# A recurrent block in 64 slots a chunk: turns, statistics and outputs at other slots, and the next chunk's normalising on ScalarE

## The reference

```python
xn = layernorm(x)                                   # over 512, eps 1e-5
q, k, v = xn @ Wq.T, xn @ Wk.T, xn @ Wv.T           # 128 wide
# per step t:  r_t = q_t @ M.T;  M = 0.99 * M + v_t.T @ k_t / 4
s = (r @ Wo.T) * sigmoid(gate)
h = layernorm(xn) * gamma + beta
y = silu(h @ dequant(fc1_q, fc1_scales) + b1)       # 512 -> 2048, scales per group of 128
z = y @ dequant(fc2_q, fc2_scales) + b2             # 2048 -> 512
g = silu(xn + 0.5 * z)
out = x + s * g
```

## Time and profile before

| | before |
|---|---|
| median of 3 runs | 1263.76 us (1263.1 to 1264.02) |
| the profiled execution | 1263.97 us, its span 1262.1 us |
| PE busy | 1196.1 us, 95% |
| DVE busy | 1135.1 us, 90% |
| ACT busy | 916.6 us, 73% |
| POOL busy | 777.7 us, 62% |
| chain that ended last | PE 77%, DVE 10%, ACT 7%, issue 4% |
| granted PE clock | 0.985 of full speed over the span |

### The profile page before, as it was taken

The page is one execution under the profiler, slowest core; times in us unless marked ns, Lnnn a source line. Parts: engine busy times, 40 slices in busy tenths (PEclk is TensorE's granted clock), DMA queues, the critical chain, the costliest instruction groups (busy, mean ns, idle before and its releaser), DMA issues.

```text
span 1262.1 us, 18951 instructions
## 1 busy us (share of the span) xinstructions
PE 1196.1 (95%) x6028; PEld 618.3 (49%) x6028; DVE 1135.1 (90%) x1965; ACT 916.6 (73%) x1590; POOL 777.7 (62%) x766
## 2 busy tenths in 40 slices
PE   2799999999999999999999999999999999999994
PEld 1344555545555554555555455555545545555551
DVE  7799899999998999999898999999898999999887
ACT  6688677777767777776777777777786777778673
POOL 6067747749474783947569384765947477494732
PEclk9799999999999999999999999999999999999997
DMA  9511130402103030120302112040210304020011
GB/s 331 182 35 34 26 76 1 101 1 65 37 15 86 1 94 8 49 53 3 99 1 68 34 38 64 1 100 2 67 34 20 82 1 101 1 59 9 26 43 35
DMA packets 41620, 65.68 MB, mean 52 GB/s; under 512 B 11696, under 2 KB 11952, under 8 KB 41008
## 3 DMA queue, kind: packets, MB, share of 16 engines
q1 hardware_dynamic: 41232, 64.36, 19.1%
q10 hardware_dynamic: 288, 0.08, 0.0%
HBM read 47.59 MB, written 16.81 MB: 51 GB/s over the span
## 4 chain that ended last, share of the span: by engine, by line
PE 77%; DVE 10%; ACT 7%; issue 4%; POOL 1%; DMA 1%; SPq 0%; ACTq 0%; DVEq 0%
PE blk L492 29%; PE blk L510 27%; PE side L452 6%; PE side L477 4%; PE side L441 3%; DVE blk L772 3%; ACT blk L638 2%; PE side L428 2%; DVE g_lo L742 2%; DVE tops L810 1%; ACT z_rows L664 1%; DVE y_split L763 1%; DVE y_split L758 1%; PE side L470 1%; PE side L471 1%
## 5 line engine op out<-in xcount | busy, mean ns | idle before, releaser
L772 DVE TENSOR_TENSOR blk<-blk,ratio_rows 128x512 f32<-128x512 f32 x960 | 647.8, 690 | 109.8 <-PE blk L510 101.0
L638 ACT ACTIVATE blk<-blk,ratio 128x512 f32<-128x512 f32 x768 | 510.0, 665 | 258.6 <-PE blk L492 250.1
L492 PE MATMUL blk<-h_split,q_sb 128*128 128x512 f16 x2048 | 612.5, 381 | 11.7 <-ACT blk L638 5.0
L510 PE MATMUL blk<-w_sb,y_split 128*128 128x512 f16 x2048 | 610.4, 380 | 4.9 <-POOL w_sb L1085 1.9
L510 PEld LDWEIGHTS blk<-w_sb,y_split 128*128 128x128 f16 x2048 | 198.9, 98 | 254.2 <-issue 12.9
L492 PEld LDWEIGHTS blk<-h_split,q_sb 128*128 128x128 f16 x2048 | 193.5, 98 | 229.9 <-issue 36.8
L645 ACT ACTIVATE y_full<-blk,par,last 128x512 f32<-128x512 f32 x256 | 200.7, 784 | 54.7 <-PE blk L492 54.3
L763 DVE SCALAR_TENSOR_TENSOR y_split<-y_full,up,y_split 128x512 f16<-128x512 f32 x256 | 224.3, 876 | 0.0
L1076 POOL CAST h_split<-h_full 128x512 f16<-128x512 f32 x64 | 42.6, 665 | 252.8 <-ACT h_full L594 252.7
L758 DVE TENSOR_SCALAR y_split<-y_full,up 128x512 f16<-128x512 f32 x256 | 152.5, 596 | 0.0
L1064 POOL TENSOR_SCALAR g_rows<-xt,mv,gs 128x512 f32<-128x512 f32 x60 | 130.7, 2187 | 0.0
(11 more groups left out here) (155 smaller groups left out, 1133.0 us busy)
## 6 DMA issues: line engine op xcount, KB each, us to landing
xt<-in_x SPq DMA_DIRECT2D x64, 256.0 KB, 4.8
x_again<-in_x SPq DMA_DIRECT2D x256, 64.0 KB, 1.9
out<-z_rows SPq DMA_DIRECT2D x256, 64.0 KB, 1.7
w_sb<-in_q SPq DMA_DIRECT2D x4, 1024.0 KB, 13.8
ratio_rows<-ratio_dram SPq DMA_DIRECT2D x4, 1024.0 KB, 9.0
y_split<-in_q SPq DMA_DIRECT2D x1, 1024.0 KB, 10.3
h_split<-in_q SPq DMA_DIRECT2D x1, 1024.0 KB, 12.6
z_rows<-in_q SPq DMA_DIRECT2D x1, 1024.0 KB, 14.2
```

What stands on the lines that cost most here:

```text
L492: mm = pe.matmul(blk[J % 2][:], q1_sb[:, g, j // 4, w, j % 4 * P:(j % 4 + 1) * P], a[:, c % 2, g, :], start=(g == 0 and n == 0), stop=(g = ...
L510: mm = pe.matmul(blk2[:, i, :], y[:, J % Y_RING, rows], w2_sb[:, j, part, :], start=(j == 0 and n == 0), stop=(j == FB - 1 and n == len(te ...
L638: act.activation(blk[J % 2][:], blk[J % 2][:], ACT.Copy, scale=ratio1[:, at:at + 1]).then_inc(blk_scaled, 1)
L772: dve.tensor_tensor(blk2[:, i, :], blk2[:, i, :], ratio2_rows[:, j, :], ALU.mult).then_inc(blk2_scaled, 1)
```

## The change

- The turns move from slots 52, 54, 56, 59 to 46, 50, 54, 58.
- The statistics of the next chunk move from slots 0 to 3 to 10, 14, 18, 22, the moments from 5, 6 to 26, 27, and the row scales from slot 7 to 28.
- Preparing, adding z, the gate's silu and the output move some four slots ahead.
- The normalising of the next chunk goes from GpSimd to ScalarE, in the same slots 36, 38, 40, 42, behind the slot's other work but for `gate_silu`. It is written as x * gs + g_shift, so that GpSimd's row scales have two steps more in each chunk. Chunk 0's own normalising stays on GpSimd.

```diff
-ROW_STEPS = 10
-FIRST_SHIFT_STEPS = 2
+ROW_STEPS = 12
-TURN_AT = (52, 54, 56, 59)
+TURN_AT = (46, 50, 54, 58)
-GATE_AT = (16, 17, 21, 29)
-
-STATS_AT, MOMENTS_AT = (0, 1, 2, 3), (5, 6)
+GATE_AT = (12, 13, 17, 25)
+
+STATS_AT, MOMENTS_AT = (10, 14, 18, 22), (26, 27)
 NORMALISE_AT = (36, 38, 40, 42)
-PREPARE_AT, ROWS_AT, FIRST_ROWS_AT = (0, 3, 15, 18), 7, 28
+PREPARE_AT, ROWS_AT, FIRST_ROWS_AT = (0, 3, 11, 14), 28, 28
-ADD_AT, OUT_AT = (13, 14, 17, 20), (18, 22, 26, 30)
+ADD_AT, OUT_AT = (9, 10, 13, 16), (14, 18, 22, 26)
...
+            def normalise(c, i):
+                if i == 0:
+                    act.wait_ge(rows_done, c + 1)
+                    act.wait_ge(turn_done, 4 * c)
+                act.activation(g_rows[:, i, :], xt[:, i, :], ACT.Identity, bias=g_shift[:, c % 2, i:i + 1],
+                               scale=gs[:, c % 2, i:i + 1]).then_inc(g_done, 1)
...
+                c, e = divmod(G, STEPS)
+                if c < NCH - 1 and e in NORMALISE_AT:
+                    normalise(c + 1, NORMALISE_AT.index(e))
                 if at := finishing(G, GATE_AT, LAST_GATE_AT):
                     gate_silu(*at)
...
+                step(pool.tensor_tensor(t[3], mean, gs[:, parity, :], ALU.mult))
+                step(pool.tensor_tensor(g_shift[:, parity, :], t[3], row_const[:, MINUS_ONE, :], ALU.mult))
                 if c == 0:
-                    step(pool.tensor_tensor(t[3], mean, gs[:, parity, :], ALU.mult))
-                    step(pool.tensor_tensor(first_shift[:], t[3], row_const[:, MINUS_ONE, :], ALU.mult))
                     for i in range(NT):
-                        first_normalise(i)
+                        normalise(0, i)
...
-            def normalise(c, i):
-                if i == 0:
-                    pool.wait_ge(rows_done, c + 1)
-                    pool.wait_ge(turn_done, 4 * c)
-                pool.tensor_scalar(g_rows[:, i, :], xt[:, i, :], mv[:, c % 2, i, 0:1],
-                                   gs[:, c % 2, i:i + 1], ALU.subtract, ALU.mult).then_inc(g_done, 1)
...
-                if c < NCH - 1 and e in NORMALISE_AT:
-                    normalise(c + 1, NORMALISE_AT.index(e))
```

More of the change, by code:

```diff
@@ L242, in build @@
         gs = sb("gs", [P, 2, NT], F32)
-        first_shift = sb("first_shift", [P, NT], F32)
+        g_shift = sb("g_shift", [P, 2, NT], F32)
         v2 = sb("v2", [P, 4, NT], F32)
@@ L1013, in link, with normalise @@
                 pool.wait_ge(pool_link, links[0])
-            def first_normalise(i):
-                pool.tensor_scalar(g_rows[:, i, :], xt[:, i, :], gs[:, 0, i:i + 1], first_shift[:, i:i + 1],
+            def normalise(c, i):
+                pool.tensor_scalar(g_rows[:, i, :], xt[:, i, :], gs[:, c % 2, i:i + 1], g_shift[:, c % 2, i:i + 1],
                                    ALU.mult, ALU.add).then_inc(g_done, 1)
@@ L1025, in rows @@
                 t = [v2[:, n, :] for n in range(4)]
-                count = [ROW_STEPS * c + (FIRST_SHIFT_STEPS if c > 0 else 0)]
+                count = [ROW_STEPS * c]
                 def step(ins):
```

## The result

The changed kernel takes 1297.05 us (median of 4, 1296.06 to 1297.49) against 1263.43: ratio 1.0264, interval 1.0247 to 1.0282, 33 us slower. The forecast was 1284 with a range up to 1296: the direction is right, the size is 13 us short.

A forecast was written before the change was run, and what follows sets the result against it. TensorE's waits bound the kernel. Gates -0.68, normalising +0.68, turns +0.53, slot 63 -0.05, VectorE +1.0 make +1.5 us a chunk, +21 over fourteen, less 1 in the last: 1284 us, range 1264 to 1296.

The forecast's parts named there:

- Bound: Whole kernel: TensorE, busy 95% of the span, bounds it; other engines count only where TensorE waits for them.
- normalising: Slots 36 to 42 on ScalarE: pairs of 43 and 45 start 0.51 and 0.17 late, +0.68 us a chunk.
- turns: Turns 50 and 54 wait for g_low, 0.74 and 0.87 us, against 0.74 and 0.34 before: +0.53 a chunk.
- slot 62: End of chunk: the wait for ScalarE's silu, 0.33 us at slot 63 before, becomes 0.28.
- Gates: Gates at 12, 13, 17, 25: losses at slots 18, 19 and 31 go but for 0.04, -0.68 us a chunk.
- Slot 24: Slots 24 and 27: statistics overfill VectorE, making y_low and remember late; 1.3 us lost against 0.27, +1.0 a chunk.
- rival 2: VectorE isn't late at 24 and 27, as GpSimd's operations and shared-port waits shift: 1267 us, chance 0.22.
- Slot 0: Start of each chunk: the forecast sum had no loss here, 0 us.
- Chunk 0: First chunk: ScalarE's extra 2.8 us against GpSimd freed for q2_low, put at 0 (+-2) us.
- the last chunk: Final chunk: has no turns and no statistics, so it gains 1 us.
- GpSimd's rows: Row scales at 28 end near 610.6, hidden by 1.4 us before slot 36; a rival had them late, 1298, 0.13.
- rival 3: Faster: turn waits at their floor, little lost to normalising, none at 24 and 27: -0.5 a chunk, 1255 us, 0.10.

The follow-up runs named there:

- norm_on_pool: The changed kernel with the normalising back on GpSimd in slots 36 to 42, still with g_shift: 1286.47 us.
- outputs_back: The changed kernel with prepare, add_z, gate_silu and output back in their slots of before: 1296.56 us.
- stats_back: The changed kernel with the next chunk's statistics and moments back in slots 0 to 3 and 5, 6: 1299.22 us.
- outputs_late_stats_back: The changed kernel with outputs at 24, 34, 38, 42 and the statistics back in slots 0 to 3: 1293.37 us.
- outputs_late: The changed kernel with the outputs at 24, 34, 38, 42 in place of 14, 18, 22, 26, gates as changed: 1286.23 us.
- last_turn_59: The changed kernel with the last turn one slot later, turns at 46, 50, 54, 59: 1289.98 us.
- changed_y_first: The changed kernel with y_high and y_low ahead of block2_out on VectorE: 1282.71 us.
- turns_5_apart: The changed kernel with the turns at 45, 50, 55, 59 in place of 46, 50, 54, 58: 1274.68 us.
- y_first: The kernel before with turns 46, 52, 56, 59, gates 15, 17, 21, 31, last output at 32, and y_high, y_low ahead of block2_out: 1233.26 us.

## Why the prediction was right and wrong

**Bound, normalising, turns, slot 62: right, sum and place.** TensorE's waits were the thing to count. The queue for ScalarE gave 0.51 and 0.17, and the trace has 0.51 and 0.18. GpSimd's freed time came back nowhere that norm_on_pool shows, with the reservation made there. The turns gave 0.74 and 0.87 as worked out.

**Gates: right in the parts, and without profit.** The 0.72 went. But outputs_back shows that the move of the outputs with them costs what they give, through slot 24.

**Slot 24: size nearly right (1.14 for 1.3), by luck, as the cause was wrong.** The step that failed is "In their new place VectorE has no room" with "`remember` ends at 602.28 + 1.2 - 0.35": it added the statistics to VectorE's queue and held its waits inside y operations fixed. It also put part of the loss at `wo` of 27, which loses nothing. stats_back took the statistics out and the loss grew; in the changed kernel's last chunk, with none, it is 1.03. Timelines of a steady chunk show why. The changed kernel, VectorE and GpSimd, with slot 24 at 612.50:

```profile
611.30 0.96 DVE L767 TENSOR_SCALAR y_split<-y_full,up 128x512 f16<-128x512 f32 x1
```
```profile
610.71 1.27 POOL L1122 TENSOR_TENSOR z_rows<-z_rows,s_rows 128x512 f32<-128x512 f32 x1
```

The same two in stats_back, with slot 24 at 613.34:

```profile
611.70 1.55 DVE L767 TENSOR_SCALAR y_split<-y_full,up 128x512 f16<-128x512 f32 x1
```
```profile
611.71 1.26 POOL L1122 TENSOR_TENSOR z_rows<-z_rows,s_rows 128x512 f32<-128x512 f32 x1
```

`y_high` takes 0.96 and 1.55 instead of 0.47, and ends 0.28 after GpSimd's product both times. Measured from slot 24, VectorE reaches it 0.44 earlier without the statistics, yet it ends 0.15 later, as GpSimd's product does, and 0.15 is what the loss grew by. A VectorE that comes earlier waits longer. What decides is which GpSimd operation stands beside `y_high` of 20 and `y_low` of 21, and the outputs' slots set that. The prediction named it, in rival 2 ("a lottery of phases"), and took it for scatter around a sum of work. The statistics aren't free either: where the outputs are out of the way they cost slot 24 0.31 (outputs_late_stats_back), and with the outputs where they were before at most 0.18 (outputs_back), against the +1.0 of the sum.

That GpSimd's outputs cause the greater part of the loss is shown by outputs_back and outputs_late. That the wait is for the ports is argued, from such rows and from the Trainium skill. The Trainium skill (SBUF — State Buffer, "Who interferes with whom") has VectorE's two-port modes contend with GpSimd, and its instructions with two SBUF inputs with a GpSimd instruction that reads SBUF; in a two-port mode whoever issues second is blocked until the first is through. The changed kernel's trace agrees: of its 512 y operations 128 are longer by a quarter or more, and every one of these ends 0.28 to 0.29 (`y_high`) or 0.54 to 0.55 (`y_low`) after a GpSimd operation that ran beside it. The kernel before shows that not every GpSimd operation blocks: 29 `y_high` lie wholly inside one of the 2.07 us normalisings (L1064), and 28 of them took 0.47 to 0.48. As far as `y_high` falls under the rule, the measurement differs from it there. This is also a reason why taking that work off GpSimd gave VectorE little; that reason is argued, not tested.

**Slot 0: missing from the sum.** The failed step is "Slot 63 keeps the same `g_high`/`h_whole`": it looked at ScalarE alone and gave the end of the chunk no term for VectorE. Turn 58 puts its `g_low` in slot 61, ahead of `y_low` of 61, whose fc2 pair stands three slots on; with the turn at 59 it was behind. There `y_low` also meets `h_low` and takes 1.47 for 0.74. last_turn_59 and changed_y_first, by two different edits, bring it ahead of both, and in each the 0.69 goes. 14 x 0.69 is 10 of the missing 13 us. I had listed fc2's three slots for odd columns in reading slot 24 and didn't walk through the other slots where they apply: 0, 8, 16, 32, 40, 48, 56.

**Chunk 0 and the last chunk.** Chunk 0, "I put at 0", was +3. In turns_5_apart it is 2.7 shorter and in norm_on_pool 0.9, so it is probably the same two causes in a chunk where ScalarE has no room. Some tenths of each are scatter: slot 24 of chunk 0 begins anywhere from 68.4 to 69.8 us in the sixteen profiles. The last chunk was to gain 1 for want of statistics and lost 0.8, by the two y waits. Against this the steady chunk's 24 and 27 were 0.16 too high.

**Rivals.** GpSimd's rows were in time for slot 36: g_shift was ready at 626.81 and ScalarE's first normalising began at 628.39. Rival 2 had the mechanism of slot 24 but expected it to take the loss away, and rival 3 didn't come.

**Open.** Of the 1.14 at slot 24, outputs_late takes 0.71 off, all of it in the length of two y operations, and the statistics make 0.31 of what is left. This holds for that order of removal only: with the outputs in place the statistics are worth nothing, since either fills the wait of the other. At slot 0 no run takes the wait beside `h_low` away and leaves the place behind `g_low`. y_first beats the sum of its parts (13 for turns and gates, 5 for the order, 30 together) by some 12 us. Its table accounts for them: the spread turns and gates uncover 0.66, 0.26 and 0.13 of VectorE's lateness, which the order then takes. How the three share the gain wasn't tested singly.

## What to carry to other kernels

In a schedule written out by slots, list for each operation on a shared engine how many slots its user is away, and give the place ahead in the slot to the one with the fewest. Here `y_low`, three slots ahead of its user, stood behind a product with four; turning them round gave 5 us alone and 17 on top of the spread turns and gates. A wait that a move takes away uncovers the next one, so price a move by walking the whole chunk, on every engine, and not the piece around the edit. And work moved to an engine that is 73% busy on average costs by the slots where it lands: 2.8 us in slots 36 to 42 lost 0.69.

## What the runs showed of the hardware

The length of VectorE's y operations is set by GpSimd. `y_high` took 0.47 to 1.56 us in the changed kernel and, where it was long, ended 0.28 to 0.29 after the GpSimd operation beside it; `y_low` took 0.74 to 1.48 and ended 0.54 to 0.55 after it. So taking work off VectorE didn't make it earlier (stats_back, 1.30 lost for 1.14). Which GpSimd operation it is matters: the 2.07 us normalising of the kernel before left 28 of the 29 `y_high` inside it at 0.47 to 0.48. On GpSimd x * gs + g_shift took 0.77 us for 128x512 (norm_on_pool), (x - mean) * gs 2.07 (before). ScalarE wasn't disturbed by any of this: its normalising took 802 to 835 ns in all 60 cases.
